# Layout of the hidden state h in a GCN + LSTM kernel: from (t, 8 batches) to (4, t, 2 batches)

## What is computed

```python
h = maximum(layernorm(x), 0)
# two graph convolutions: h = relu(adj @ (h @ Wg + bg))
# then, for p = 1, 2, 3, 4: the sequence is cut into windows of p positions,
# an LSTM with its own weights runs over each window from a zero state,
# and its last hidden state replaces position p-1 of that window (in place, so p+1 sees it)
x = x + h
h = maximum(layernorm(x), 0)
# x + diag(adj) h W0 + triu(adj, 1) h W1 + tril(adj, -1) h W2 + bias
```

## Time and profile before

| | |
|---|---|
| median of 3 runs | 469.38 us |
| lowest, highest | 469.1, 469.44 us |
| profiled execution, first to last instruction | 469.0 us |
| TensorE matmul, busy | 435.9 us (93%) |
| VectorE, busy | 351.5 us (75%) |
| ScalarE, busy | 288.4 us (61%) |
| GpSimd, busy | 65.9 us (14%) |
| granted TensorE clock, mean | 0.967 |

### The profile page before, as it was taken

One profiled execution on the slowest core, in us unless ns is written; L12 is line 12 of the kernel. 1 busy time (PEld: TensorE's weight loads), 2 busy tenths in 40 slices (PEclk: granted clock), 3 DMA queues, 4 the chain that ended last, 5 costly groups with the idle time before them and its releaser, 6 DMA issues.

```text
span 469.0 us, 7895 instructions
## 1 busy us (share of the span) xinstructions
PE 435.9 (93%) x2602; PEld 388.1 (83%) x2602; DVE 351.5 (75%) x859; ACT 288.4 (61%) x568; POOL 65.9 (14%) x59
## 2 busy tenths in 40 slices
PE   3988898999879999999978999999988899999997
PEld 3766698997758899999756889999876789999987
DVE  5488879974996788885789678888499777768751
ACT  5686666652766576772575666766186666767252
POOL 4760020001320002000132002000034000000150
PEclk9998989998999999998899999999799999999899
DMA  7800000000001000000000000000000000000011
GB/s 217 345 1 1 1 0 1 1 1 0 1 12 41 11 1 13 17 1 2 0 1 17 34 11 12 0 17 1 0 0 2 34 7 11 1 18 0 2 56 57
DMA packets 6080, 11.16 MB, mean 24 GB/s; under 512 B 1056, under 2 KB 4768, under 8 KB 5536
## 3 DMA queue, kind: packets, MB, share of 16 engines
q1 hardware_dynamic: 6048, 10.77, 6.6%
HBM read 6.57 MB, written 4.19 MB: 23 GB/s over the span
## 4 chain that ended last, share of the span: by engine, by line
issue 58%; PE 20%; DVE 7%; POOL 7%; ACT 4%; DMA 2%; SPq 1%; DVEq 0%; ACTq 0%; POOLq 0%
PE PS L494 4%; POOL RS L300 3%; PE PS L443 2%; PE PS L439 2%; PE PS L440 2%; ACT H L626 2%; DMA WH<-whh_t 2%; DVE HL L762 2%; PE PS L483 2%; DVE CS L775 1%; PE PS L456 1%; PE PS L453 1%; PE PS L452 1%; DVE H L837 1%; POOL WIL L320 1%
## 5 line engine op out<-in xcount | busy, mean ns | idle before, releaser
L664 ACT ACTIVATE GT<-PS,BG 128x256 f32<-128x256 f32 (+2 forms) x312 | 159.3, 563 | 58.5 <-PE PS L456 31.8
L439 PE MATMUL PS<-HH,WIH 128*128 128x256 f32 (+2 forms) x312 | 109.9, 352 | 12.9 <-DVE HL L762 5.0
L443 PE MATMUL PS<-HL,WIH 128*128 128x256 f32 (+2 forms) x312 | 105.0, 336 | 0.5
L440 PE MATMUL PS<-HH,WIL 128*128 128x256 f32 (+2 forms) x312 | 104.3, 334 | 0.0
L300 POOL TENSOR_TENSOR RS<-VE,NHALF 128x8 f32<-128x8 f32 (+2 forms) x15 | 26.5, 1769 | 363.0 <-DVE VE L732 363.0
L439 PEld LDWEIGHTS PS<-HH,WIH 128*128 128x128 f32 x312 | 59.9, 192 | 20.4 <-issue 6.6
L673 ACT ACTIVATE TC<-CS 128x512 f32<-128x512 f32 (+2 forms) x88 | 45.1, 513 | 50.2 <-DVE CS L784 30.0
L803 DVE TENSOR_TENSOR HT<-GT,TC 128x512 f32<-128x512 f32 (+2 forms) x88 | 47.9, 544 | 27.4 <-ACT TC L673 26.1
L443 PEld LDWEIGHTS PS<-HL,WIH 128*128 128x128 f32 x312 | 59.9, 192 | 7.5 <-DVE HL L812 3.2
L494 PEld LDWEIGHTS PS<-WL,UK 128*128 128x128 f32 x384 | 52.1, 195 | 13.1 <-DVE X L855 6.5
L440 PEld LDWEIGHTS PS<-HH,WIL 128*128 128x128 f32 x312 | 59.9, 192 | 3.3
(11 more groups left out here) (74 smaller groups left out, 666.3 us busy)
## 6 DMA issues: line engine op xcount, KB each, us to landing
X<-x_tbd SPq DMA_DIRECT2D x3, 1024.0 KB, 12.2
out_tbd<-X SPq DMA_DIRECT2D x15, 192.0 KB, 1.9
X<-x_tbd SPq DMA_DIRECT2D x4, 256.0 KB, 4.2
WI<-wih_t SPq DMA_DIRECT2D x1, 1024.0 KB, 6.5
out_tbd<-X SPq DMA_DIRECT2D x7, 128.0 KB, 1.7
WH<-whh_t SPq DMA_DIRECT2D x1, 768.0 KB, 8.0
out_tbd<-X SPq DMA_DIRECT2D x1, 256.0 KB, 2.0
WL<-w_l SPq DMA_DIRECT2D x1, 192.0 KB, 7.3
```

What stands on the lines that cost most here:

```text
L439: pe.matmul(dst, WIH[:, p - 1, cols], x_high, start=True, stop=False)
L440: pe.matmul(dst, WIL[:, p - 1, cols], x_high, start=False, stop=False)
L443: mm = pe.matmul(dst, WIH[:, p - 1, cols], x_low, start=False, stop=(j == 0))
L664: act.activation(GT[:, s, q, 0:n], bank(s, q)[:, 0:n], ACT.Tanh if q == C else ACT.Sigmoid, bias=BG[:, 4 * (p - 1) + q:4 * (p - 1) + q + 1 ...
```

## The change

h is kept as (4, t, 2 batches): batch number n of the stream lies at (n % 4, t, n // 4). One batch with all t is now single elements 8 bytes apart. The windows of position j are runs of 2 elements, one run each p x 8 bytes, four times over (for p = 1 the runs join to four of 128 elements). The columns of gates, cells and hidden states follow in the order (4, window, 2). PACK is 4, HBANKS is 2, HB is 8.

```diff
-        HH = sb("HH", [128, STREAMS, T, HB], F32R)
-        HL = sb("HL", [128, STREAMS, T, HB], F32R)
+        HH = sb("HH", [128, STREAMS, PACK, T, HBANKS], F32R)
+        HL = sb("HL", [128, STREAMS, PACK, T, HBANKS], F32R)
...
             first = p * w0 + j
-            return h[:, s, first:first + p * (nw - 1) + 1:p, :]
+            return h[:, s, :, first:first + p * (nw - 1) + 1:p, :]
+
+        def as_windows(ap):
+            return ap.rearrange("p (o w i) -> p o w i", o=PACK, i=HBANKS)
...
-                    dst = bank(s, q)[:, 0:n].rearrange("p (w b) -> p w b", b=HB)
+                    dst = as_windows(bank(s, q)[:, 0:n])
...
-                    pe.matmul(dst, HH[:, s, :, n], IDENTR[:, :], start=True, stop=False)
+                    pe.matmul(dst, HH[:, s, n % PACK, :, n // PACK], IDENTR[:, :], start=True, stop=False)
...
-                    mm = pe.matmul(dst, HL[:, s, :, n], IDENTR[:, :], start=False, stop=True)
+                    mm = pe.matmul(dst, HL[:, s, n % PACK, :, n // PACK], IDENTR[:, :], start=False, stop=True)
...
-                    act.activation(HH[:, s, :, n * PACK:(n + 1) * PACK].rearrange("p t b -> p b t"),
-                                   as_batches(bank(s, n)), ACT.Relu).then_inc(h_high, 1)
+                    act.activation(HH[:, s, :, :, n], as_batches(bank(s, n)), ACT.Relu).then_inc(h_high, 1)
...
-                    part = slice(n * PACK, (n + 1) * PACK)
-                    dve.scalar_tensor_tensor(out=HL[:, s, :, part].rearrange("p t b -> p b t"),
-                                             in0=as_batches(bank(s, n)), scalar=0.0,
-                                             in1=HH[:, s, :, part].rearrange("p t b -> p b t").bitcast(F32),
+                    dve.scalar_tensor_tensor(out=HL[:, s, :, :, n], in0=as_batches(bank(s, n)), scalar=0.0,
+                                             in1=HH[:, s, :, :, n].bitcast(F32),
...
                     return (windows(HH, s, p, j, w0, nw), windows(HL, s, p, j, w0, nw),
-                            HT[:, s, 0:n].rearrange("p (w b) -> p w b", b=HB))
+                            as_windows(HT[:, s, 0:n]))
```

## The result

The changed kernel takes 549.84 us (median of 4 runs, 548.21 to 550.57), the kernel before 469.41 us beside it. The ratio is 1.171, 95% interval 1.168 to 1.174. The forecast was 556 us. The profile is of the 548.21 us execution, whose mean granted clock was 0.981; the other three had 0.988 to 0.991.

A forecast was written before the change was run, and what follows sets the result against it. TensorE's stream of columns was taken to set the pace. From the median 469.4: + 116.4 (matmuls) - 8 (cover) - 15.4 (transposes) - 6 (making h) + 0 (clock) = 556.4, so 556 us; range 439 to 590.

The forecast's parts named there:

- Part 4: Window matmuls L439, L440, L443: TensorE's moving operand pays 1.75 ns per run of two, 116.4 us lost over four groups.
- the equal price of a far element on three engines: Far element costs 2.02 ns on VectorE, 1.89 on ScalarE, 1.85 in weight loads; read as a memory time.
- The sign at the low clock: 512-column matmuls take 0.4275 us at 1.2 GHz, nothing over; at 2.4 GHz something besides the array holds the operand up.
- the 19 ns over the columns: 512-column matmuls at 2.4 GHz: interval 0.2325 us where the columns make 0.213, counted as a sign against rival A.
- Idle time that covers: TensorE's idle time and low clock at changes of window length: slower matmuls of the other stream cover 8 us.
- Part 1: Transposes (L467, L470): pairs with closer weight loads go at 0.117 us, 128 x 0.120 = 15.4 us gained.
- Part 2: Making h (L619, L762): ScalarE's and VectorE's writes get cheaper, 1.5 us in each of 4 groups, 6 us gained.
- Part 5: Granted clock after the transposes: 9 us back if falls stop, set against new falls: 0, ends -9 and +25.
- the same kind of thin work: Half-rate matmuls through p = 2 to 4 may bring new clock falls, at 2 us or so each.
- Rival A: A run of two is enough for the moving operand, under 0.91 ns a pair at L440: 448 or 439 us; chance 0.27.
- B: Rival: half the moving operand's penalty, because reads of neighbouring runs overlap in part: 502 us; chance 0.07.
- C: Rival: transposes' 0.237 us is a short matmul's price and pairs are free: 463 to 469 us; chance 0.03.

The follow-up runs named there:

- the run with single elements: The changed kernel with h laid out as (8 batches, t), so windows are single elements 8, 12 and 16 bytes apart: 550.74 us (one run).
- the fp32 run: The changed kernel with the first of the three window matmuls (L442) in fp32 in place of fp32r: 641.18 us (one run).
- The making of h: The kernel before with the loops of L619 and L762 turned round, t outside and the 4 batches inside: 466.47 us, ratio 0.994.

## Why the prediction was right, and where it was not

**Part 4** carried the sign and the size. Measured excess at the full clock: 42 x 0.2195 + 66 x 0.144 + 90 x 0.113 = 28.9 us a group, 115.6 us in all, against 116.4. The choice between 0.91 and 1.85 ns for a run of two rested on the equal price of a far element on three engines. The number came out, 0.451 us for 256 runs, 1.76 ns each, but in part by luck, because the reason was only half right. Against it stands the run with single elements: on the moving port a far element costs 0.90 ns, not 1.8, and a pair costs 1.8 as two elements that do not fill their group. That an engine slower than 0.45 ns an element hides the loss was right, by the fp32 run. The sign at the low clock pointed the right way, but the 19 ns over the columns say nothing of runs: the flat tiles of L455 to L459 stand 0.23 us apart too. After the first stall of the changed kernel the clock is at 0.50, and the pairs do not notice:

```profile
36.43 0.63 PE L443 MATMUL PS<-HH,WIL 128*128 128x512 f32 x1
...
41.87 0.63 PE L443 MATMUL PS<-HH,WIL 128*128 128x512 f32 x1
```

```profile
37.00:41.50 4.50, 4.50 (x12) 3.07 (x11) 3.15 (x8) 3.10 (x5) 0.00 (x0) 0.50 0.00 0
43.00:49.50 6.50, 6.50 (x15) 2.90 (x14) 3.48 (x8) 1.88 (x3) 0.00 (x0) 1.00 0.00 0
```

5.44/12 = 0.453 us at 1.2 GHz and 0.451 at 2.4 GHz. The price does not move with the array's clock; that it is one of fetching the operand is my reading of this, and no run looks inside it.

**Idle time that covers.** I took 8 us. The LSTMs grew by 103.4 us for 115.6 us of matmuls: 12.2 do not show, 6.1 in group 0 and about 2 in each other group. In group 0 TensorE's idle time shrank by 2.6 us, from 6.5 to 3.9. Most of the rest is low clock, of which the sum had named 2 us: the kernel before loses some 3.5 us to it there (0.95 over 73.5 us), and pairs lose nothing to it.

**Part 1** was right in the price (0.118 us a pair, 15.1 us in all) and in the place for three groups. The 0.117 us had a weaker source than it seemed: L395 is an fp32 matmul with two records, so the row has 32 records of 16 matmuls, and 0.117 is half a matmul, not a pair of load and matmul as in the transposes. It came out all the same. In the last group the same 3.8 us, with a fall of the clock that went too (0.64 from 440 to 444 us in the kernel before), brought only 1.9: behind those transposes the tail goes on to VectorE and GpSimd (the chain of the changed kernel runs over L819, L826, L303, L837), which the sum did not look at. The changed kernel, and then the kernel before:

```profile
523.34 4.30 DVE L837 TENSOR_SCALAR H<-X,MINUS,RS 128x128 f32<-128x128 f32 x8 [1.15 <-POOL RS L303]
524.88 2.42 POOL L360 TENSOR_TENSOR X<-X,BIAS 128x1024 f32<-128x1024 f32 x1 [1.58 <-ACT H L628]
527.72 2.35 POOL L360 TENSOR_TENSOR X<-X,BIAS 128x1024 f32<-128x1024 f32 x1 [0.42 <-DVE H L837]
527.75 2.88 DVE L843 TENSOR_SCALAR H3H<-H 128x1024 fp32r<-128x1024 f32 x1
...
446.83 2.14 DVE L837 TENSOR_SCALAR H<-X,MINUS,RS 128x128 f32<-128x128 f32 x8 [0.40 <-POOL RS L300]
449.08 0.69 DVE L843 TENSOR_SCALAR H3H<-H 128x1024 fp32r<-128x1024 f32 x1
```

VectorE needs 7.2 us in place of 2.8 for the same work on the chain, and it does so where GpSimd's bias add runs beside it. In the kernel before that add starts at 449.93 us, behind both. All five traces in which the tail's transposes are fast have this overlap and the long instructions, and the other seven have neither. So 4.3 us of what the transposes gave were lost in these two lines; that the add beside them is the cause is my reading, as no run moved it away.

**Part 2** was 1.0 us at the start and, after the transposes' 3.8 and the clock's 3.1 us, about 0.8 us of the 7.7 between the groups: some 3.4 us where 6 stood. L622 takes 0.64 us and L763 0.68, as forecast, but only the first stream's wait was on the path: the second's (0.58 us at 126.64 in the kernel before) goes too, and TensorE then waits 1.9 us in place of 1.06 for ScalarE's copy of the last layer.

**Part 5** is the term that failed. Its 9 us are more than the 6 us between forecast and result: the 4 us by which the cover was set too low go the same way, and what parts 1 and 2 failed to bring (1.9 us in the tail, 2.6 us) goes the other, so the forecast is closer than its terms. I let new falls of the clock cancel what the transposes give back. The falls between the groups went, and their 9 us came back in full. New falls did come. The changed kernel has three that the kernel before has not:

```profile
93.30:96.70 3.40, 3.40 (x16) 3.40 (x15) 2.71 (x9) 2.31 (x4) 0.00 (x0) 0.50 0.00 0
144.40:147.90 3.50, 3.44 (x10) 2.74 (x11) 3.12 (x10) 2.10 (x4) 0.00 (x0) 0.52 0.00 0
277.60:281.10 3.50, 3.50 (x12) 2.60 (x12) 3.47 (x12) 1.74 (x4) 0.51 (x1) 0.51 0.00 0
```

The last two, some 1.7 us each, stand at p = 1, where h is read whole, behind waits of TensorE of 1.9 us. The first stands among half-rate matmuls of p = 4, 1.7 us after a wait of 0.6 us, and costs next to nothing, since these take 0.237 us there and 0.233 at full clock. Elsewhere matmuls at half rate did not pull the clock down: from 425 to 455 us, all at p = 2 and 3, it is 1.00:

```profile
425.00:455.00 30.00, 30.00 (x92) 17.70 (x91) 15.81 (x27) 15.46 (x26) 0.00 (x0) 1.00 0.01 3
```

So "the same kind of thin work" is not borne out for p = 2 to 4 as a whole; what part the half-rate matmuls have in the one fall at 93.3 us stays open.

**Rival A** fell by the number it named: 0.91 ns for a pair, where 1.76 was measured. B wanted half of that excess and C none of the loads' gain, and neither is in the rows. The Trainium skill's rule of two hits on a 16-byte line ("SBUF — State Buffer", "SBUF: two separate sides") agrees with the loads (two elements a line: 0.119 us, one: 0.237), and nearly with ScalarE and VectorE (two: 0.639 and 0.684 us, one: 1.135 and 1.133, whole, as in the run "The making of h": 0.592 and 0.683). On the moving operand of an fp32r matmul the trace does not agree: two elements a line go at half rate, and only whole lines go at the full one. Its 16 bytes do show, in the run with whole runs of four 8 bytes further on.

## What to carry to other kernels

Lay out the moving operand of an fp32r matmul in aligned runs of four elements of 4 bytes; single elements and pairs doubled the time of the elements concerned. Pairs were enough for weight loads, ScalarE and VectorE, and nearly so for an fp32 matmul, which is slow by itself. When the profile gives a matmul's count or distance, check by the code how many records one matmul leaves. When a layout must be poor for someone, let it be for the operand with the fewest elements: here 128 transposes of 128 elements against 267,000 columns. Try the order of the loops first, since PSUM could be read with a stride for nothing, and slow transposes mixed with other matmuls kept the clock up between groups in the one execution that was traced. And follow a gain behind TensorE: in the tail here most of it was lost on VectorE, beside GpSimd.

## What was not expected of the hardware

- A lone element 16 bytes from the next costs the moving operand as much as each element of a pair, 0.90 ns (0.23 us for 256 columns), while a lone element costs a weight load 1.85 ns.
- With half of the elements in whole groups the cost is about half the excess (0.349 us between 0.2325 and 0.451), so it is settled group by group and not for the instruction.
- ScalarE and VectorE read PSUM with 512 bytes from element to element at full rate (592 and 683 ns for 512 elements).
- An fp32 matmul leaves two records in the profile, takes 0.86 us for 512 whole columns and 0.90 us with pairs, while fp32r goes from 0.23 to 0.45.
- VectorE's L843 takes 2.88 us beside GpSimd's bias add and 0.69 us without it.
